# Two AdaLN blocks with a routed expert stage: the order of one table and the filler rows on GpSimd

## The reference

```python
logits = xf @ gate_w.T                       # experts 4 to 7 are excluded
weights = jax.nn.softmax(logits, axis=-1)
top_w, top_idx = jax.lax.top_k(weights, 2)
top_w = top_w / jnp.sum(top_w, axis=-1, keepdims=True)
cw = jnp.zeros((T, E)).at[jnp.arange(T)[:, None], top_idx].add(top_w)
h = silu(einsum('td,edh->teh', xf, w1)) * einsum('td,edh->teh', xf, w3)
out = einsum('te,ted->td', cw, einsum('teh,ehd->ted', h, w2))
x = x + gb * out
```

## Time and profile before

| | |
|---|---|
| median of 3 runs | 1836.85 us (1833.61 to 1837.3) |
| profiled execution, its own time | 1853.13 us |
| its span, first to last instruction | 1851.3 us |
| mean granted TensorE clock | 0.877 |
| busy | PE 1484.3 us (80%), DVE 1319.1 (71%), POOL 786.8 (43%), ACT 759.7 (41%) |
| `wring<-w_all`, weights | 201 DMAs |
| `blk<-queue`, blocks | 67 DMAs |
| `acc<-ys,blk` (L944) | 134 DMAs |

### The profile page before, as it was taken

The page is one execution under the profiler, slowest core; times in us unless marked ns, Lnnn a source line. Parts: engine busy times, 40 slices in busy tenths (PEclk is TensorE's granted clock), DMA queues, the critical chain, the costliest instruction groups (busy, mean ns, idle before and its releaser), DMA issues. The chain is left out here.

```text
span 1851.3 us, 38699 instructions
## 1 busy us (share of the span) xinstructions
PE 1484.3 (80%) x11601; PEld 1174.7 (63%) x11601; DVE 1319.1 (71%) x2888; ACT 759.7 (41%) x1627; POOL 786.8 (43%) x1324
## 2 busy tenths in 40 slices
PE   3457777789898989898888888898888989882784
PEld 2235454577676767676676767676767767672773
DVE  5667768697978787887779686878878874541442
ACT  1332634545453544535253535445353625240220
POOL 1000142445454546353545444463535453636432
PEclk7667878899999999989798988999999988796887
DMA  6231313364646363636355553636363737552775
GB/s 191 77 119 62 109 64 97 130 205 150 208 149 209 122 209 105 209 134 189 134 167 180 155 186 118 216 105 202 132 201 126 223 127 210 176 170 89 246 229 166
DMA packets 205216, 291.44 MB, mean 157 GB/s; under 512 B 35840, under 2 KB 167936, under 8 KB 200864
## 3 DMA queue, kind: packets, MB, share of 16 engines
q1 hardware_dynamic: 172176, 251.01, 40.4%
q0 software_dynamic: 25824, 27.74, 7.2%
q10 hardware_dynamic: 7088, 11.29, 1.7%
HBM read 215.26 MB, written 70.91 MB: 155 GB/s over the span
## 5 line engine op out<-in xcount | busy, mean ns | idle before, releaser
L944 POOL DMA_INDIRECT acc<-ys,blk x134 | 225.6, 1684 | 443.5 <-issue 220.0
L1822 PE MATMUL bank<-xs_hi,wring 128*128 128x256 f32 x804 | 280.2, 348 | 71.8 <-DVE xs_lo L1509 54.5
L1462 DVE TENSOR_REDUCE mneg<-bank 128x2 f32<-128x512 f32 (+1 forms) x384 | 236.4, 684 | 37.1 <-PE bank L1705 32.2
L1824 PE MATMUL bank<-xs_lo,wring 128*128 128x256 f32 x804 | 241.3, 300 | 1.4 <-issue 1.4
L1823 PE MATMUL bank<-xs_hi,wring 128*128 128x256 f32 x804 | 241.7, 301 | 0.4 <-issue 0.4
L1822 PEld LDWEIGHTS bank<-xs_hi,wring 128*128 128x128 f32 x804 | 167.3, 208 | 114.5 <-DVE xs_lo L1509 49.4
L1838 PE MATMUL y_ps<-wring,h 128*128 128x128 f32 (+1 forms) x1608 | 235.1, 289 | 5.2 <-DVE h L1530 5.2
L1838 PEld LDWEIGHTS y_ps<-wring,h 128*128 128x128 f32 (+1 forms) x1608 | 206.5, 196 | 30.4 <-issue 11.6
L1131 ACT ACTIVATE arena<-bank 128x512 f32<-128x512 f32 x384 | 197.8, 607 | 50.3 <-PE bank L1705 39.3
L807 POOL TENSOR_TENSOR rstd_a<-ve_a,mhalf 128x4 f32<-128x4 f32 x48 | 54.7, 1139 | 328.5 <-DVE ve_a L1341 324.9
L1179 ACT ACTIVATE tt<-bank 128x512 f32<-128x512 f32 x201 | 120.0, 597 | 165.3 <-PE bank L1824 105.8
(11 more groups left out here) (253 smaller groups left out, 3003.2 us busy)
## 6 DMA issues: line engine op xcount, KB each, us to landing
wring<-w_all SPq DMA_DIRECT2D x201, 640.0 KB
blk<-queue SPq DMA_DIRECT2D x67, 272.0 KB
q_stack<-q_rows SPq DMA_DIRECT2D x16, 1024.0 KB
k_stack<-k_rows SPq DMA_DIRECT2D x16, 1024.0 KB
rows<-mod_rows SPq DMA_DIRECT2D x32, 384.0 KB, 5.4
q_rows<-qk_halves SPq DMA_DIRECT2D x48, 256.0 KB
k_rows<-qk_halves SPq DMA_DIRECT2D x48, 256.0 KB
w_all<-wring ACTq DMA_DIRECT2D x4, 1536.0 KB, 6.8
```

Source lines behind the costliest of these rows:

```text
L944: send(g.indirect_dma_start(acc, bass.IndirectOffsetOnAxis(ap=blk[:, b, t, IDCOL:IDCOL + 1].bitcast(I32), axis=0), ys[:, b % 2, t, :], Non ...
L1462: frees(v.tensor_reduce(dst, ps.bank(use)[:].rearrange("p (h k) -> p h k", k=P if name[0] == "A" else S), AX, ALU.max, negate=True), use)
L1822: mm(dst[:, at], w_hi[:, w], xs_hi[:, b % 2, :], start=True, stop=False)
L1824: last = mm(dst[:, at], w_hi[:, w], xs_lo[:, b % 2, :], start=False, stop=True)
```

## The change

Where the filler rows are sent is moved from behind the scatter of the last pair (turn 14) to behind the table of group 14 (the same turn). Nothing else is changed.

```diff
-            def scatter_and_flush(it):
-                scatter(it)
-                if it.reg is None and it.plus == PAIRS - 1:
+            def table_and_flush(it):
+                make_table(it)
+                if it.reg is None and it.plus == PAIRS - 2:
                     flush()
 
             turns(pool, pool_order, dict(stats1=stats1, stats2=stats2, stats3=stats3, stats4=stats4, modulate4=modulate4, route=route,
-                                         scatter=scatter_and_flush, table=make_table, add_rows=add_rows))
+                                         scatter=scatter, table=table_and_flush, add_rows=add_rows))
```

## The result

The changed kernel took 1825.84 us (median of 4 executions, 1825.13 to 1828.4) beside 1835.86 us of the kernel before (4, 1833.61 to 1837.3): ratio 0.9949, 95% interval 0.9932 to 0.9966, that is 10.0 us less, where 4.4 were forecast and 1829.0 was the lower end.

What follows compares the result with a forecast made beforehand. From landing A to the end the chain of accumulating stores was taken to bound the kernel, not TensorE. Gains of 0.6 + 2.1 (A) + 1.7 (B) + 0 (C) = 4.4 us gave 1836.85 - 4.4 = 1832.4 us, range 1829.0 to 1837.4.

Steps and rivals of the forecast that it cites:

- A: Landing of the accumulating stores add_rows (13,1), which ys of block (13,3) waits for: forecast at 1710.3, 2.7 us earlier.
- B: Landing of add_rows (13,2), which releases block (14,2): forecast at 1716.5, 4.4 us earlier.
- C: Landing of add_rows (13,3), which releases add_rows (14,0): forecast 4.4 us earlier.
- third rival: Only the load mattered: VectorE's order does not hold xs_lo back, 11.8 us come through, 1825.1 us; chance 0.04.
- the signs of that rival: In VectorE's order, xs_lo of block (14,0) would start before ys of block (13,3).
- start of the add: GpSimd's start of add_rows (13,1), behind table and filler: forecast at 1704.65, 0.6 us earlier.
- The row of 421 GB/s: Rate taken for weights alone, by which 4.4 MB of filler, weights and block take 10.4 us, until 1708.2.
- the step from A to B: From landing (13,1) to landing (13,2): 7.91 us before, forecast 6.2 us because the weights are through sooner.
- B to C: From landing (13,2) to landing (13,3), beside the weight reloads: taken unchanged at 11.35 us.
- the four reloads: SP's reloads of four weight units, said to be freed by TensorE's down products: forecast 3.2 us earlier.
- the first rival: The shadow moves with the loads: A takes its 7.69 us, B its 7.91, only 0.6 gained, 1836.2 us; chance 0.30.
- the 16.3 us between profiled execution and median: Amount by which the runs' median lies below the profiled time, taken off 1853.13 to give the base 1836.85 us.

Runs made afterwards that it cites:

- e3: Changed kernel with the filler's adds, cast and stores moved behind add_rows (13,1), (13,2) and (13,3): 0.9950 of the kernel before, 1827.92 us.
- e4: Changed kernel with VectorE's product of block (13,3) put behind xs_lo of block (14,0): 0.9985 of the kernel before, 1833.54 us.
- e9: Kernel before, filler still ahead of the table, with only add_rows (13,1) moved ahead of both: ratio 0.9959, 175.6 us behind the last scatter.
- e10: Changed kernel, nothing edited, timed once more against the kernel before: ratio 0.9975, 1834.03 beside 1839.88 us.
- e5: Changed kernel with SP holding weight units 1 to 4 of group 14 back until the filler has landed: 0.9990 of the kernel before, 1830.24 us.
- e6: Changed kernel with add_rows (13,1) ahead of table (14) and the filler behind adds (13,2) and (13,3): 0.9929 of the kernel before, 1820.96 us.

## Why the prediction was right and wrong, point by point

**What bounds the kernel: right.** The gain followed the landings A, B and C and not the load for which TensorE was seen to wait; e3, e4 and e9 each part the two and agree. The first measurement, 1825.84 us, lies next to the 1825.1 of the third rival, for which the load was all that mattered. That is chance: `ys` still stood ahead of `xs_lo` and waited for A, as forecast, and the signs of that rival are absent.

**The terms**, as means of four traces each, earlier than before by: start of the add 0.5 us (forecast 0.6); start of (13,2), which is A, 2.1 (2.7); of (13,3), B, 4.5 (4.4); of (14,0), C, 5.0 (4.4); end 4.4 (4.4). A was oversized. The stream of weights and filler ran at 363 GB/s at first and not at 421, so it ended over 1 us behind the pair's issue, the pair's packets had to wait behind the filler's in their queue, and the landing took 6.2 us in place of 5.6. (The row of 421 GB/s was not weights alone, as the prediction has it: add_rows (13,2) falls into that window.) B came out right because two errors cancelled: A came 0.6 us too late, but the step from A to B, now 6.0 us (forecast 6.2), had taken 8.4 us in the mean of the four traces of before and not the 7.91 of the one read. C was undersized: B to C took 10.2 to 10.8 us in three traces in place of the 11.35 taken over, though 12.4 in e10, longer than the 11.35 that the prediction had named as a sign of being wrong. Behind C the changed kernel's traces take 0.6 us more on average than those of before, where nothing was to change.

**The reloads beside C: a wrong reading that did no harm.** The prediction ties the four reloads to TensorE's down products and lets them come 3.2 us earlier. But SP sends them right behind its load of block (14,2), which waits for landing B. In the kernel before SP's timeline has the two blocks (14,1) and (14,2), then the reloads; the changed kernel's lines above show the same, 0.27 us apart:

```profile
1713.17 8.30 SPq L690 DMA_DIRECT2D blk<-queue  x2
```

So the reloads start with B, 4.5 us earlier in the mean of four traces each. C comes when they are through, in either program. Windows around C, before (1732.22) and changed (1708.68):

```profile
1731.00:1732.00 1.00, 1.00 (x11) 1.00 (x10) 0.46 (x1) 0.18 (x1) 0.00 (x0) 1.00 0.62 240
1732.00:1733.00 1.00, 1.00 (x9) 0.88 (x8) 0.55 (x1) 0.42 (x1) 0.02 (x1) 1.00 0.03 10
...
1707.00:1708.00 1.00, 1.00 (x11) 1.00 (x11) 0.46 (x1) 0.21 (x1) 0.00 (x0) 1.00 0.89 324
1708.00:1709.00 1.00, 1.00 (x12) 1.00 (x11) 0.58 (x1) 0.38 (x1) 0.00 (x0) 1.00 0.21 82
```

In all eight traces of the two programs the last packet of the reloads ends within 0.5 us of C, and both came 4.9 to 5.0 us earlier with the change. The Trainium skill ("DMA: Bandwidth & Descriptors", queues, rings and completion order) has a semaphore's increment land only after every earlier write of its DMA engine, across the queues, and these traces agree with that; the 3.2 us that the prediction worked out by it came from the wrong start of the reloads. No run moves the reloads alone, so that C waits for them is read from the traces and not shown by an experiment.

Of the first rival (the shadow moves with the loads) e5 showed the mechanism, by holding the weights: 1.2 us of gain left at the end.

**The predicted time and its range: wrong, against the first measurement.** 1832.4 us were forecast and 1825.84 measured, 6.6 less. The mechanism and the 4.4 us hold, so the step that failed is the term for scatter between executions: "over 1 us of the runs' own spread", on the median of three executions within 3.7 us. 1.0 us of the 6.6 is that base, as the set of four had a median of 1835.86. The other 5.6 are the difference of 10.0 us in place of 4.4, and most of it (4 to 5 us) did not come back in the longer comparisons and the traces. The part ahead of the change, in which no instruction differs, takes 1646.7 to 1673.6 us, and medians of the unchanged kernel were 1835.9, 1837.4, 1833.0 and 1839.9 us in four sets, on more than one chip. The range should have had room for 5 us of that on either side of the forecast. Likewise the 16.3 us between profiled execution and median, which the prediction takes over with "I take the same difference off it", were no constant of the profiler: this execution had two of the long turns on its way to the scatter, and the changed kernel's profiled execution lay 2.6 us above its median.

**Open.** How much of the first comparison's 10.0 us beyond some 5 is chance can't be told from it; three comparisons of twelve executions of the changed kernel each (4.2 to 7.3 us between medians) and eight traces (4.4 to 5.2) say that the change itself is worth about 5. Why single turns ahead of the scatter take 6 us more, and whether the change has any part in it, was not settled.

## What to carry to other kernels

Ending a wait of 29 us for a load is worth only what the next thing missing allows: ask of every engine that idles across the same gap what it waits for, and in what order its list has the two. Where indirect accumulations follow each other by a wait on the one before, they are the chain, and small work of the issuing engine goes behind them, into their landing times (e6: 9 us more than the change brought by the traces, 4.7 by the medians, with the same instructions). To price an edit of 0.2%, compare the stretch that it touches, counted from a common point ahead of it, in several traces; totals scatter by more than the effect.

## What the runs showed of the hardware that was not expected

An accumulating pair landed 5.2 us after its start with little else in the DMA engines (e5), 6.2 at the end of a full stream, 7.7 with the stream starting beside it, and 9.5 to 11.6 beside the reloads, whose end it then met within 0.5 us (C, in the eight traces of the two programs). With the weights beside it, the last of the filler's stores moved 4.5 us behind the end of its issue, and the add behind it in GpSimd's queue moved only then. And one program took 1787.7 us in one comparison and 1833 to 1840 in the others; the one trace from there (e9) has the difference ahead of the last scatter, where a turn of the loop takes 93 to 96 us in place of 97 to 99.5.
